# Start of a quantised graph-layer kernel: constants and one subtraction on GpSimd, one copy on VectorE, and x's first rows on SyncE's queue

## What is computed

```python
h = relu(layernorm(x))
w = quantise((weight - mean(weight)) / std(weight), wgt_alpha, 3 bits)   # one mean and std over 512 x 512
s = relu(quantise(h, act_alpha, 4 bits) @ w)
x = x + adj @ quantise(s, act_alpha2, 4 bits)
h = relu(layernorm(x))
x = x + second_layer(h, adj)     # reduces to h itself unless an off-diagonal pair meets adj == 1
```

## Time and profile before

| | us |
|---|---|
| median of 3 runs (lowest to highest) | 152.13 (152.08 to 152.52) |
| profiled execution, its own time | 151.76 |
| its span, first to last instruction | 150.0 |
| TensorE busy | 136.5 |
| VectorE busy | 108.2 |
| ScalarE busy | 103.8 |
| GpSimd busy | 33.2 |

### The profile page before, as it was taken

The page is one execution under the profiler, slowest core; times in us unless marked ns, Lnnn a source line. Parts: engine busy times, 40 slices in busy tenths (PEclk is TensorE's granted clock), DMA queues, the critical chain, the costliest instruction groups (busy, mean ns, idle before and its releaser), DMA issues.

```text
span 150.0 us, 2094 instructions
## 1 busy us (share of the span) xinstructions
PE 136.5 (91%) x678; PEld 85.9 (57%) x678; DVE 108.2 (72%) x230; ACT 103.8 (69%) x154; POOL 33.2 (22%) x64
## 2 busy tenths in 40 slices
PE   0398999999999999999999999999999999999920
PEld 0494545555555555757484757566666657579920
DVE  0989888899855569996764686686968797765450
ACT  3688957698686779407956999999999779411000
POOL 2352054344030000025100201101010652611010
PEclk9999999999999999999999999999999999999997
DMA  5999999243672880250289899998011021011102
GB/s 164 336 418 418 395 398 384 49 78 61 175 212 40 244 350 0 48 236 0 31 281 418 251 378 358 376 365 336 36 45 70 0 74 70 0 70 70 70 9 72
DMA packets 12925, 27.70 MB, mean 185 GB/s; under 512 B 6128, under 2 KB 6384, under 8 KB 10864
## 3 DMA queue, kind: packets, MB, share of 16 engines
q1 hardware_dynamic: 12624, 27.14, 51.5%
q10 hardware_dynamic: 288, 0.39, 0.8%
HBM read 22.03 MB, written 4.19 MB: 175 GB/s over the span
## 4 chain that ended last, share of the span: by engine, by line
PE 79%; issue 5%; DVE 4%; POOL 2%; ACT 1%; POOLq 0%; DVEq 0%
PE acc L1050 27%; PE acc L1046 25%; PE acc L1030 9%; PE acc L1025 9%; PE acc L1012 8%; POOL rs L571 1%; DVE st L758 1%; PE acc L998 1%; ACT h_i L433 1%; DVE ring L831 1%; DVE x_sb L955 1%; ACT z_sup L441 0%; ACT hi L399 0%; DVE w_i L839 0%; DVE h_i L784 0%
## 5 line engine op out<-in xcount | busy, mean ns | idle before, releaser
L1050 PE MATMUL acc<-sup,lo 128*128 128x512 f32 (+1 forms) x208 | 48.3, 384 | 0.0
L1046 PE MATMUL acc<-sup_h,hi 128*128 128x512 f16 (+1 forms) x208 | 43.7, 363 | 0.0
L1050 PEld LDWEIGHTS acc<-sup,lo 128*128 128x128 f32 x208 | 37.0, 188 | 7.9
L556 POOL TENSOR_SCALAR nm<-mv 128x1 f32<-128x1 f32 (+2 forms) x19 | 13.1, 692 | 98.5 <-DVE ve L768 78.6
L414 ACT ACTIVATE junk<-raw,below 128x2048 uint8<-128x2048 f32 x16 | 31.8, 1988 | 0.0
L1046 PEld LDWEIGHTS acc<-sup_h,hi 128*128 128x128 f16 x208 | 19.4, 98 | 21.4 <-issue 2.9
L813 DVE TENSOR_TENSOR lo<-raw,hi 128x2048 fp32r<-128x2048 f32 x11 | 25.2, 2288 | 7.5 <-ACT hi L406 7.5
L448 ACT ACTIVATE ring<-x_sb,nm 128x512 f32<-128x512 f32 x15 | 10.4, 715 | 20.4 <-POOL nm L556 17.2
L1030 PE MATMUL acc<-sup,lo 128*128 128x512 f32 x64 | 21.4, 446 | 0.1
L406 ACT ACTIVATE hi<-raw 128x2048 f16<-128x2048 f32 x11 | 20.8, 1895 | 0.0
L758 DVE BATCH_NORM_STATS2 st<-x_sb 128x6 f32<-128x512 f32 x29 | 19.5, 687 | 0.4
(11 more groups left out here) (76 smaller groups left out, 80.7 us busy)
## 6 DMA issues: line engine op xcount, KB each, us to landing
raw<-adj_t SPq DMA_DIRECT2D x16, 1024.0 KB, 6.2
out<-ring SPq DMA_DIRECT2D x15, 256.0 KB, 4.8
x_sb<-x SPq DMA_DIRECT2D x3, 1024.0 KB, 13.8
w_sb<-weight SPq DMA_DIRECT2D x4, 258.0 KB, 4.0
x_sb<-x SPq DMA_DIRECT2D x1, 512.0 KB, 5.6
x_sb<-x ACTq DMA_DIRECT2D x1, 256.0 KB, 3.4
x_sb<-x SPq DMA_DIRECT2D x1, 256.0 KB, 4.8
h_iT<-h_i SPq DMA_TRANSPOSE x10, 2.5
```

The source lines that it names most:

```text
L1046: nc.tensor.matmul(bank[:, cols], part(hi, k % PARTS, j), sup_h[:, j, cols], start=(j == 0), stop=False)
L1050: ins = nc.tensor.matmul(bank[:, cols], part(lo, k % PARTS, j), sup[:, j, cols], start=False, stop=(j == T - 1))
```

## The change

What it does:

- x's tile 0 is loaded by `load_x(0)` on SyncE's queue after the four weight loads, no longer on ScalarE's queue.
- The six operations of `constants` and L741 leave VectorE. GpSimd does them: three behind the first weight block's landing, `C_W` and `C_SUP` behind tile 0's inverse root, and `C_OUT0` and `C_OUT` at the end of the first phase.
- `lo` of piece 0 is made on GpSimd, behind tile 1's inverse root and ahead of the layer norm steps of tiles 2 and 3.
- `h_qT` of tile 1 is made by `bound_hT(1)` on VectorE, behind the last `clip_w` and ahead of `normalise(3, stats(3))`. ScalarE's `copy_T(1)` goes.
- ScalarE makes `hi` of piece 0 ahead of `relu_sup(0)`, no longer behind it.
- On VectorE, `normalise(4)` now stands ahead of `bound_hT(2)`, and `normalise(5)` ahead of `bound_hT(4)`; `lo_of_piece(1)` stands ahead of `stats(4)`.
- The warm-ups behind tile 0's transposes are 18, no longer 20.

```diff
-    WARM_SUMS, WARM_FIRST, WARM_T = 16, 4, (20, 0)
+    WARM_SUMS, WARM_FIRST, WARM_T = 16, 4, (18, 0)
...
             for k in range(KD):
                 load_w(k)
+            load_x(0)
             load_x(1)
...
-            act.dma_start(x_sb[:, 0, :], x[0:P, :]).then_inc(x_in[0], 16)
             sums(0)
             relu1(0)
...
             round_w(2)
             round_w(3)
-            copy_T(1)
+            split_piece(0)
             relu_sup(0)
-            split_piece(0)
             relu_sup(1)
...
+            def lo_of_piece(p):
+                pool.wait_ge(hi_piece, p + 1)
+                cols = slice(p * PIECE, (p + 1) * PIECE)
+                nc.gpsimd.tensor_tensor(lo[:, 0, cols], raw[:, 0, cols], hi[:, 0, cols],
+                                        ALU.subtract).then_inc(lo_by_pool, 1)
+            pool.wait_ge(w_in[0], 16)
+            nc.gpsimd.tensor_scalar(cc(C_IQ), scs(S_AA), 1.0 / ACT_LEVELS, None, ALU.mult).then_inc(const_part, 1)
+            nc.gpsimd.tensor_scalar(cc(C_SUP0), scs(S_AA), 1.0 / WGT_LEVELS, scs(S_WA), ALU.mult,
+                                    ALU.mult).then_inc(const_part, 1)
+            pool.wait_ge(const_part, 1)
+            nc.gpsimd.tensor_tensor(cc(C_IQ2), cc(C_IQ), cc(C_IQ), ALU.mult).then_inc(consts_ready, 1)
             pool.wait_ge(half_ready, 1)
             mean_of_sum(0)
             var_of_squares(0)
             inverse_root(0, 1)
+
+            nc.gpsimd.tensor_scalar(cc(C_W), cc(C_RWA), WGT_LEVELS, None, ALU.mult).then_inc(consts_ready, 1)
+            pool.wait_ge(const_part, 2)
+            nc.gpsimd.tensor_tensor(cc(C_SUP), cc(C_SUP0), cc(C_RAA2), ALU.mult).then_inc(consts_ready, 1)
             mean_of_sum(1)
...
             inverse_root(1, 1)
+            lo_of_piece(0)
             for n in range(EARLY + 1, FIRST + 1):
...
+            nc.gpsimd.tensor_tensor(cc(C_OUT0), cc(C_RSC), scs(S_SCALE), ALU.mult).then_inc(const_part, 1)
+            pool.wait_ge(const_part, 3)
+            nc.gpsimd.tensor_scalar(cc(C_OUT), cc(C_OUT0), 1.0 / ACT_LEVELS, scs(S_AA2), ALU.mult,
+                                    ALU.mult).then_inc(const_out, 1)
...
-            constants()
             w_stats(2)
...
-            dve.wait_ge(consts_ready, 1)
+            dve.wait_ge(consts_ready, 3)
...
+            bound_hT(1)
             normalise(3, stats(3))
             quantise_sup(0)
-            lo_of_piece(0)
             quantise_sup(1)
+            lo_of_piece(1)
             wait_x(4)
             stats(4)
-            lo_of_piece(1)
-            last = stats(5)
+            normalise(4, stats(5))
             bound_hT(2)
-            normalise(4, last)
             bound_hT(3)
             lo_of_piece(2)
             quantise_sup(2)
             stats(6)
-            last = stats(7)
+            normalise(5, stats(7))
             bound_hT(4)
-            normalise(5, last)
```

More of the change, by code:

```diff
@@ L171, in gnn_kernel @@
         qin_ready = sem("qin_ready")
+        const_part = sem("const_part")
         consts_ready = sem("consts_ready")
+        const_out = sem("const_out")
         x_summed = sem("x_summed")
@@ L192, in gnn_kernel @@
         hi_piece = sem("hi_piece")
+        lo_by_pool = sem("lo_by_pool")
         lo_piece = sem("lo_piece")
@@ L254, in wait_hT, with wait_lo_piece @@
         def wait_hT(eng, j):
-            if j < EARLY:
-                eng.wait_ge(hqT_ready, j + 1)
-            else:
-                eng.wait_ge(hqT_bounded, j - EARLY + 1)
+            if j == 0:
+                eng.wait_ge(hqT_ready, 1)
+            else:
+                eng.wait_ge(hqT_bounded, j)
+        def wait_lo_piece(eng, p):
+            if p == 0:
+                eng.wait_ge(lo_by_pool, 1)
+            else:
+                eng.wait_ge(lo_piece, p)
         def wait_hi(eng, k):
@@ L268, in wait_lo @@
             if k <= GT:
-                eng.wait_ge(lo_piece, 4 * (k + 1))
+                wait_lo_piece(eng, 4 * k + 3)
+                if k == 0:
+                    eng.wait_ge(lo_by_pool, 1)
             else:
@@ L571, in inverse_root, with cc, scs @@
                 nc.gpsimd.tensor_tensor(rs[:, a:a + m], ve[:, a:a + m], minus_half[:, 0:m], ALU.pow).then_inc(r_ready, 1)
+            def cc(i):
+                return cn[:, i:i + 1]
+            def scs(i):
+                return w_sb[:, 0, D + i:D + i + 1]
+            def lo_of_piece(p):
[9 more added lines that the diff above has]
+            nc.gpsimd.tensor_tensor(cc(C_IQ2), cc(C_IQ), cc(C_IQ), ALU.mult).then_inc(consts_ready, 1)
             pool.wait_ge(half_ready, 1)
@@ L740, in first_constants @@
                 nc.vector.tensor_scalar(cc(C_QIN), cc(C_RAA), ACT_LEVELS, None, ALU.mult).then_inc(qin_ready, 1)
[L741 to L750, removed]
             def wait_x(t):
@@ L794, in bound_hT @@
                     turned = h_iT[:, j % 2, :, :].rearrange("p k i -> p (k i)")
-                dve.wait_ge(sup_in_psum, j - 1)
+                if j >= 2:
+                    dve.wait_ge(sup_in_psum, j - 1)
                 nc.vector.tensor_scalar(h_qT[:, j % 2, :], turned, 0.0, ACT_LEVELS, ALU.max, ALU.min).then_inc(hqT_bounded, 1)
@@ L948, in _ @@
                     split_lo(GT + 1)
+            dve.wait_ge(const_out, 1)
             for s in range(GT, T + 1):
@@ L1026, in aggregate_first @@
                 pe.wait_ge(sup_ready, j + 1)
-                pe.wait_ge(lo_piece, j + 1)
+                wait_lo_piece(pe, j)
                 for t in rows:
```

## The result

The changed kernel took 154.67 us (median of 4 runs, 153.79 to 155.06) against 152.18 (4 runs): a ratio of 1.0148, 95% interval 1.0120 to 1.0175. In a second series, seven runs of it gave 153.51 against 152.12, a ratio of 1.0078 (1.0049 to 1.0106). The two intervals do not meet; the change is a loss of 1.4 to 2.5 us in the medians, and what spreads it stays partly open. The median of all eleven runs is 153.73. The profiled execution took 153.79 with a span of 151.9, 2.0 and 1.9 more than before.

A forecast was written before the change was run, and what follows sets the result against it. TensorE's matmuls bound the kernel, with a fixed length from 22 us, so only the start matters. First aggregate matmul 1.7 late, less 0.4 of waits, plus 0.1, is 1.4 us: 152.13 to 153.5, range 152.1 to 154.9.

The forecast's parts named there:

- the sum's loss: Whole path: 1.7 - 0.4 + 0.1 = 1.4 us later; chance 0.50.
- the rival with the clock on top: TensorE's clock rises late after its gap before tile 0's transposes: middle 0.8 us more, 154.3; chance 0.22.
- Tile 0's landing: Load fifth on SyncE's queue: lands at 6.7, 2.55 us later; not much under 5.8, hardly over 7.4.
- VectorE's chain: Weight's mean, variance and scale behind quantise_h(0): 1.46 us late, less 0.28 no longer waited for TensorE, is 1.18.
- ScalarE as the last to come: Tile 1's sum and the weight roundings behind tile 0's work: 2.01 us late, replacing VectorE's 1.18 on the path.
- the step from tile 0 to tile 1: ScalarE from tile 0's first sum to tile 1's: 1.88 us to the ReLU plus 0.80 for it, 6.72 to 9.40.
- The copy on VectorE: Tile 1's copy, 0.42 us, stands ahead of sup_h of tile 0; first aggregate matmul at 16.4, 1.7 later.
- Constants on GpSimd: Seven small operations leave VectorE, GpSimd takes 0.10 to 0.34 us for each: worth nothing on the path.
- The 0.2 that was let go: C_W and C_SUP on GpSimd could reach tile 1 with at most 0.2 us; taken as nothing.
- `lo` on GpSimd: lo of piece 0: 0.69 to 1.4 us, taken as 1.4, ending at 16.4, its reader coming at 17.3.
- Order and waits: After the first aggregate matmul: 0.4 us of waits go; normalise(5) ahead of bound_hT(4) costs 0.1 before support(4).
- The faster rival: Tile 0 lands before about 6.2 and work taken off the path counts for more: 151.4 us; chance 0.16.

The follow-up runs named there:

- e1: The changed kernel with tile 0's load back on ScalarE's queue, all else as changed: 151.86 us, ratio to before 0.9935.
- e2: The kernel before with only tile 0's load moved behind the weight on SyncE's queue: 153.90 us, ratio 1.0089.
- e5: The changed kernel again, unedited, beside the kernel before: 153.51 us, ratio 1.0078.
- e3: The changed kernel with 19 warm-ups in place of 4 ahead of tile 0's transposes, 22 in place of 18 behind them: 153.37 us, ratio 1.0061.
- e6: e2 with 19 warm-ups in place of 4 ahead of tile 0's transposes, 24 in place of 20 behind them: 154.24 us, ratio 1.0151.
- e12: The kernel before without the 16 and 4 warm-ups ahead of tile 0's transposes: 152.25 us, ratio 1.0014.
- e11: e1 with normalise(4) and normalise(5) in the old order and tile 1's copy back on ScalarE: 152.05 us, ratio 0.9988.
- e9: e1 with normalise(4) and normalise(5) in the old order and tiles 6 and 7 transposed on TensorE too: 151.91 us, ratio 0.9989.
- e8: e1 with normalise(4) and normalise(5) in the old order and adj's fourth chunk issued behind tile 7's DMA transpose: 153.57 us, ratio 1.0081.

## Why the prediction was right, step by step

It named a loss of 1.4 us, 153.5, with a range of 152.1 to 154.9, through tile 0's load. e1 and e2 show that cause. How near the figure is depends on the series. The second, 153.51, is on it. The first, 154.67, is 1.1 above the sum's loss, nearer to the rival with the clock on top (154.3, chance 0.22) and 0.2 inside the range. In the profile the sum's loss of 1.4 was 1.77, with terms that missed both ways. The steps:

- **Tile 0's landing** was taken at 6.7; it landed 4.5 us behind its issue at 2.60, at 7.1, and in e5 at 7.3, in e3 at 6.8, in e2 at 7.1 and in e6 at 6.7. The term is too small by 0.4 in the profiled execution, and it isn't one number.
- **VectorE's chain.** 1.46 - 0.28 = 1.18 was forecast for the weight's scale; it was 11.77 against 10.14, 1.63, which is the forecast plus the 0.4.
- **ScalarE as the last to come** holds: the last clip waited for its rounding. The size was 2.08 against 2.01, with the later landing in it, so the step from tile 0 to tile 1 was priced a little high (7.12 to 9.68 is 2.56, not 2.68), and from tile 1's sum to the rounding it took 3.06 in place of 3.27.
- **The copy on VectorE** cost 0.42, and stood where it was put. But `sup_h` waited 0.17 for the ReLU after all: `support(0)` ended near 15.6, not 14.8, with the later data and the lower clock. The first aggregate matmul was 1.93 late, not 1.7.
- **Constants on GpSimd** took 0.19 to 0.27 each, inside the bounds. `C_W` and `C_SUP` are on the chain: tile 1's mean began at 10.60 though its sum was there at 10.4. The 0.2 that was let go is real.
- **`lo` on GpSimd** took 1.16, against bounds of 0.69 and 1.4, and ended at 16.10, well ahead of its reader. The Trainium skill's factor of 1.96 (GPSIMD Engine Reference, Performance versus the Vector engine), by which it would be 1.35 (an estimate), is high for 512 columns: the row says 1.7.
- **Order and waits.** From the first aggregate matmul to tile 4's transposes it was 7.04 against 7.29: 0.25 given back, not 0.4. `normalise(5)` ahead of `bound_hT(4)` cost more than 0.1: from those transposes to `support(4)` it was 1.44 (23.68 to 25.12) against 1.13 (22.00 to 23.13), so 0.31, with TensorE 0.14 idle. The step failed in supposing that the half aggregate covers all but 0.1 of the aggregation and the variance. But then 0.21 came back by tile 6's support (30.85 against 29.07), because the kernel before had waits of its own there, among them tile 6's transpose by DMA, which a later start covers. The sum 1.93 - 0.25 + 0.31 - 0.21 = 1.78 is the loss at the last 16 matmuls, to 0.01. From there on the stretch is of fixed length, as the prediction said.
- **The clock** was put on top at 0.22 and came in the profiled execution. The profiles with a late tile 0 have spans of 151.3 (e3, e6) and 151.7 (e5) with `support` at or near 96 ns, and 151.9 (after) and 152.6 (e2) with 151 ns in it. Less the start of tile 0's first sum these are 144.4 (e3), 144.6 (e6), 144.3 (e5), 144.8 (after) and 145.5 (e2): the late clock went with some 0.4 us more in the changed kernel and 0.9 in e2, and the landing moved the rest. By the Trainium skill's TensorE: Matmul & The Clock Gate, Part 1, sustained activity releases the throttle. The traces agree in part: with a late tile 0 the clock was up before `support(0)` where the gap was filled (e3, e6) and not where it wasn't (after, e2, e5). Against it, e12 had the gap and an early rise, e11 no such gap and a late one, and no series shows a clear gain from the filling.

The faster rival failed at its landing. Its other half, that the edits taken off the path pay 0.4 or more once tile 0 is early, was right at the start, where e1's first aggregate matmul is at 14.32 and e9's at 14.30, 0.39 and 0.41 earlier, and failed at tile 6, whose transpose waits in SyncE's queue behind `adj`'s bytes. No step of the prediction had looked past 22 us for such a wall, as the chain showed TensorE alone there; it did not matter for a later start.

What stays open: why the two series of the changed kernel differ by 0.7%, how the clock behaves in the executions without a trace, and how the spread divides between the clock and the loads' landings.

## What to carry to other kernels

Ask of each load which chain waits for it, not which tensor matters more: here 256 KB moved behind 1 MB cost its landing 2.95 us, of which the covering work hid 1.2; the other 1.8, a part of it by the late clock, went through to the end. A pure TensorE chain can still be an upper bound on gains: a transpose by DMA just behind a large load was nearly late, so an earlier start won nothing, and moving that transpose (e8, e9) brought costs of its own. Where landings and the clock's rise differ from execution to execution, time the kernel in a dozen runs beside the one that it is compared with, and compare profiles from a common event, for one profile shows one landing and one rise.

## What was not expected of the hardware

On one queue the weight's first block landed 2.8 us behind its issue in place of 3.2, and its last 4.3 in place of 4.6, while the five loads together ended 0.4 us later than the five on two queues had (in e6's profile at the same 6.7). A transpose by DMA took 2.5 us in the median and 5.66 behind a 1 MB load. Behind a wait of TensorE of 2.1 us the granted clock fell to 0.50 for over 2 us (e8). The twelve runs of e12 lie in two groups, seven and five, with 0.7 us between them.
